# DLRM interaction tower on one core: the gathers of each feature group wait for a step of TensorE

## The chip, the core and the metric

The kernel runs on one core of a Trainium2 chip. The metric is the device time of one execution in microseconds (us), lower is better; the median of three runs is given. Engines: TensorE (PE) multiplies matrices, with its weight loads shown apart (PEld); VectorE (DVE), ScalarE (ACT) and GpSimd (POOL) work elementwise; SyncE (SP) and ScalarE also issue plain DMAs, and GpSimd issues the indirect ones, the gathers.

## The reference

For each of 2048 samples, 27 embedding rows of 128 floats are looked up, all pairs of them multiplied, and the result goes through a small MLP:

```python
e = jnp.stack([tbl_0[ids[:, 0]], ..., tbl_26[ids[:, 26]]], axis=1)   # (2048, 27, 128)
inter = einsum('bfd,bgd->bfg', e, e)                                  # 27 x 27 per sample
x = inter[:, lower triangle]                                          # 351 pairs
h = concatenate([bottom, x, bottom], axis=1)                          # (2048, 607)
h = maximum(h @ W_top1 + b_top1, 0)                                   # 512
h = maximum(h @ W_top2 + b_top2, 0)                                   # 256
y = h @ W_top3                                                        # (2048, 1)
```

The tables have 1000 to 125000 rows. Everything is float32.

## The kernel before

The 2048 samples are 16 tiles of 128, and two tiles make a half (256 samples, `h` from 0 to 7; the name is the kernel's). Tile `t` of half `h` is `2h` (even) or `2h + 1` (odd).

The ten smallest tables (1000 or 1250 rows) lie in SBUF, split in a rounded part `tab_hi` and a rest `tab_lo`. Their rows are not gathered but selected: VectorE builds a one-hot matrix from the indices (`one_hot`, line 536), TensorE multiplies the table's chunk with it (`select`, line 389). A **step** is one chunk of one set of tables, that is one one-hot and its 4 or 8 matmuls, and TensorE counts it in the semaphore `onehot_used`. Half 0 has 50 steps (sets of two tables or one), each later half 26 (two sets of four tables with 8 chunks, 8 matmuls a step; one set of two tables with 10 chunks, 4 matmuls a step), 168 selection matmuls in all. `OH_AT[h]` is the count of steps ahead of half `h`. Five one-hots can be ahead of TensorE.

The other 17 tables are gathered from HBM by GpSimd, one indirect DMA per tile and feature (128 rows of 512 bytes), 272 in all (line 359). The 17 features are in five groups of 3, 3, 4, 3, 4 (`GROUPS`), with first features 0, 3, 6, 10, 13. The buffer `emb` has two slots, so tile `t` goes where tile `t - 2` was, and group `g` of it waits until TensorE has transposed group `g` of tile `t - 2` (`is_filled(pool, "rows", t - TILE_SLOTS, g)`, line 357). Within GpSimd the gathers are issued strictly in order.

TensorE's program is an order written out by hand (from line 474). For a half from 2 on: the first two sets of `select` (128 matmuls); the transposes of the even tile, groups 0 to 3 (`rows`, line 401); the third set (40 matmuls); group 4; the transposes of the bottom input (line 425); layer 2 of the MLP for half `h - 2` (lines 459 to 461); the Gram products of the even tile (`products`, line 416, four steps of 32 matmuls, each counted in `grammed`); layer 3 for half `h - 2` (line 470); the transposes of the odd tile, groups 0 to 4; layer 1 for half `h - 1` (lines 442 to 444, 48 matmuls); the Gram products of the odd tile. The semaphore `filled` counts in this same order each bank of PSUM that TensorE has filled. Half 7 has no layer 1 in its place; the last layers follow the end of its Gram products.

ScalarE copies the selected and transposed rows to `embT` (lines 506 and 675) and the Gram products to `inter` (line 683); SyncE stores them to HBM and loads them back packed by pairs (lines 319 and 280). In half 0 the tables and weights are loaded and split, which ScalarE (642, 647) and VectorE (521, and 542 to 562 for the weights) do between the steps.

Of the kernel before, what the change touches and what calls it, by code (L numbers as in the profile page):

```python
# [34 lines left out]
def dlrm_tower(nc, bottom, ids, sel_ids, gather_tables, select_tables, w_top1, b_top1, w_top2, b_top2, w_top3, out):  # L35
# [20 lines left out]
    for f in range(1, NF):  # L56
        k, g = f * (f - 1) // 2, 0
        while g < f:
            n = min(f - g, P - k % P)
            PACKS.append((f, g, n, k // P, k % P))  # L60
            k, g = k + n, g + n
# [14 lines left out]
    for rows in shapes:  # L76
        of_shape = [i for i in range(NSEL) if select_tables[i].shape[0] == rows]
        FOURS += [(of_shape[a:a + 4],) + table_chunks(rows) for a in range(0, len(of_shape), 4)]
    K = FOURS[0][1]
    assert all(k == K for _, k, _ in FOURS) and all(four[-1] - four[0] == len(four) - 1 for four, _, _ in FOURS)  # L80
    CHUNKS = [table_chunks(t.shape[0])[1] for t in select_tables]
    CHUNK_AT = [sum(CHUNKS[:i]) for i in range(NSEL)]

    TWOS = [(four[a:a + 2], k, chunks) for four, k, chunks in FOURS for a in range(0, len(four), 2)]
    TWOS = TWOS[:1] + TWOS[-1:] + TWOS[1:-2] + [([i], k, chunks) for four, k, chunks in TWOS[-2:-1] for i in four]
    TABLE_ORDER = [i for two, _, _ in TWOS for i in two]


    PIECE = BANK // D
    PIECES = [(TABLE_ORDER.index(i), a, min(PIECE, CHUNKS[i] - a)) for two, _, chunks in TWOS for a in range(0, chunks, PIECE) for i in two]  # L90
    SPLIT_BY = [max(p for p, (x, _, _) in enumerate(PIECES) if x == n) + 1 for n in range(NSEL)]
    PIECES_OF = [[p for p, (n, _, _) in enumerate(PIECES) if TABLE_ORDER[n] in two] for two, _, _ in TWOS]
# [3 lines left out]
    OH_AT = [sum(len(one) for one in ONEHOTS[:h]) for h in range(HALVES + 1)]  # L96
    ROW_IDS = sorted({c for _, _, c in FOURS})
    ROW_AT = {c: sum(x for x in ROW_IDS if x < c) for c in ROW_IDS}
    GRAMS = P // QUADS // SPAN
# [64 lines left out]
    with ExitStack() as ctx:  # L164
# [3 lines left out]
        def sem(name):  # L168
            return ctx.enter_context(nc.semaphore(name))
# [74 lines left out]
        onehot_used = sem("onehot_used")  # L244
        filled = sem("filled")
        freed = [sem(f"freed_{b}") for b in range(BANKS)]
        grammed = sem("grammed")
# [15 lines left out]
        def is_filled(eng, *key):  # L263
            eng.wait_ge(filled, fill[key])
# [11 lines left out]
        def load_packs(eng, h, packs, loaded):  # L276

            both = grams[2 * h:2 * h + 2].rearrange("t s f g n -> (t s) f g n")
            for f, g, n, c, k in packs:
                eng.dma_start(packed[k:k + n, c, :].rearrange("k (s n) -> k s n", s=2 * QUADS),  # L280
                              both[:, f, g:g + n, :].rearrange("s k n -> k s n")).then_inc(loaded[c], 16)
# [60 lines left out]
        @block.gpsimd  # L342
        def _(pool):
            for c in ROW_IDS:
                pool.iota(row_id[:, ROW_AT[c]:ROW_AT[c] + c], pattern=[[1, c]], base=0, channel_multiplier=c).then_inc(row_id_ready, 1)
            pool.wait_ge(ident_zeroed, 1)
            pool.affine_select(out=ident[:, :], in_=ident[:, :], compare_op=ALU.not_equal, fill=1.0,
                               base=0, pattern=[[-1, P]], channel_multiplier=1).then_inc(ident_ready, 1)
            pool.wait_ge(ids_loaded[0], 16)
            for t in range(TILES):  # L350
                if t == 2:
                    pool.wait_ge(ids_loaded[1], 16)
                if t == ID_SLOTS:
                    pool.wait_ge(ids_loaded[2], 16)
                for g, features in enumerate(GROUPS):
                    if t >= TILE_SLOTS:
                        is_filled(pool, "rows", t - TILE_SLOTS, g)
                    for f in features:
                        pool.indirect_dma_start(  # L359
                            out=emb[:, t % TILE_SLOTS, f, :], out_offset=None, in_=gather_tables[f],  # L360
                            in_offset=bass.IndirectOffsetOnAxis(ap=ids_all[:, t % ID_SLOTS, f:f + 1].bitcast(U32), axis=0),
                        ).then_inc(gathered[t % TILE_SLOTS][g], 16)
            pool.wait_ge(packed_split, CH * (HALVES - 1))
            pool.wait_ge(stored, 16 * QUADS * TILES)
            load_packs(pool, HALVES - 1, POOL_PACKS, packs_pool)
# [447 lines left out]
```

## Time and profile before

| | |
|---|---|
| median of 3 runs | 382.04 us (380.87 to 382.43) |
| span of the profiled execution | 633.3 us |
| TensorE busy, in the profile | 402.0 us (63%), 4321 matmuls |
| TensorE weight loads | 374.0 us (59%) |
| VectorE | 254.0 us (40%) |
| ScalarE | 144.4 us (23%) |
| GpSimd | 262.1 us (41%) |
| mean granted TensorE clock | 0.827 of full |
| DMA | 45.76 MB, mean 72 GB/s |

No time from outside the profiler is listed for the profiled execution itself; its own time is the span of 633.3 us, which is 251 us longer than the median of the timed runs. So no share of the span may be taken for a share of the 382 us. A row of the timeline gives start, duration, engine, line, operation, output and inputs, and in brackets how long the engine was idle before and what ended that. "issue" there means that the engine waited for nothing that the profile shows.

### The profile page before, as it was taken

The numbers are of one execution on the slowest core, as the hardware profiler recorded it, in microseconds if no ns is written. First come the engines' busy times: TensorE is split into PE (matmuls) and PEld (weight loads), VectorE is DVE, ScalarE is ACT, GpSimd is POOL, SyncE is SP. The second block draws the span as 40 slices with busy tenths as digits, with TensorE's granted clock in tenths as the row PEclk, the third lists the DMA queues.
The fourth block names the chain that finished last, engine by engine and source line by source line (L and its number), as shares of the span: only waits on it lengthen the run. The fifth ranks groups of instructions, "written<-read, shape, count | busy, mean of one in ns | idle before, by whom it ended". The sixth has DMA issues, their size and how long they took to land.

```text
span 633.3 us, 10256 instructions
## 1 busy us (share of the span) xinstructions
PE 402.0 (63%) x4321; PEld 374.0 (59%) x4321; DVE 254.0 (40%) x341; ACT 144.4 (23%) x268; POOL 262.1 (41%) x283
## 2 busy tenths in 40 slices
PE   2207655492738928298465956469392892839997
PEld 2206543492727918197464955469381992829986
DVE  3117955191315704074040921338040560407422
ACT  3204722020302213112311123012130221311521
POOL 6761447317370364505463073712646045550010
PEclk9999967597668969599595996769776896959999
DMA  8812652114221232114121241211321132211021
GB/s 200 174 50 77 175 167 77 52 28 135 55 55 40 64 104 65 41 40 128 35 75 28 45 134 47 61 39 36 127 64 53 36 81 84 64 40 39 9 61 9
DMA packets 44889, 45.76 MB, mean 72 GB/s; under 512 B 32720, under 2 KB 35558, under 8 KB 43948
## 3 DMA queue, kind: packets, MB, share of 16 engines
q1 hardware_dynamic: 33646, 26.52, 16.3%
q0 software_dynamic: 8896, 17.89, 10.9%
q10 hardware_dynamic: 2302, 0.70, 0.5%
q8 instruction: 34, 0.56, 0.4%
q14 instruction: 11, 0.09, 0.0%
HBM read 39.52 MB, written 5.55 MB: 71 GB/s over the span
## 4 chain that ended last, share of the span: by engine, by line
PE 50%; issue 20%; another core or an unknown queue 18%; ACT 5%; DVE 4%; DMA 2%; SPq 0%; ACTq 0%; DVEq 0%
PE work L389 21%; PE gram L416 16%; PE work L401 3%; PE work L442 2%; PE work L443 2%; PE work L444 2%; DVE onehot L536 2%; ACT embT L506 2%; ACT embT L675 2%; DMA inter<-in_tbl 1%; PE work L470 1%; DVE tab_lo L521 1%; DMA misc<-in_bottom 1%; PE work L459 1%
## 5 line engine op out<-in xcount | busy, mean ns | idle before, releaser
L359 POOL DMA_INDIRECT emb<-in_tbl,ids_all x272 | 258.2, 949 | 304.9 <-PE work L401 217.7
L536 DVE TENSOR_TENSOR onehot<-ids_bc,row_idf 125x1024 fp32r<-125x1024 int32 (+2 forms) x232 | 199.4, 921 | 94.0 <-PE work L389 60.9
L416 PE MATMUL gram<-embT 128*54 128x52 f32 x2048 | 110.3, 264 | 161.7 <-issue 134.6
L389 PE MATMUL work<-onehot,tab_hi 125*128 125x256 f32 x672 | 172.8, 296 | 51.2 <-DVE onehot L536 26.0
L416 PEld LDWEIGHTS gram<-embT 128*54 128x54 f32 x2048 | 93.9, 179 | 181.5 <-issue 164.2
L389 PE MATMUL work<-onehot,tab_lo 125*128 125x256 f32 x672 | 169.2, 291 | 0.0
L389 PEld LDWEIGHTS work<-onehot,tab_hi 125*128 125x128 f32 x672 | 133.8, 199 | 57.0 <-DVE onehot L536 32.4
L389 PEld LDWEIGHTS work<-onehot,tab_lo 125*128 125x128 f32 x672 | 134.3, 200 | 0.0
L675 ACT COPY embT<-work 128x512 f32<-128x512 f32 (+1 forms) x41 | 30.4, 795 | 163.5 <-PE work L389 98.9
L569 DVE SCALAR_TENSOR_TENSOR x_lo<-work,x_hi 128x512 fp32r<-128x512 f32 x16 | 11.0, 691 | 103.9 <-ACT x_hi L708 72.6
L683 ACT COPY inter<-gram 118x416 f32<-118x416 f32 x64 | 32.3, 506 | 66.5 <-remote 33.6
L506 ACT COPY embT<-work 128x512 f32<-128x512 f32 (+1 forms) x64 | 36.4, 623 | 25.8 <-remote 16.5
L708 ACT ACTIVATE x_hi<-work 128x512 fp32r<-128x512 f32 x14 | 8.4, 597 | 144.7 <-remote 129.9
L442 PE MATMUL work<-x_hi,w_hi 128*128 128x256 f32 (+1 forms) x128 | 36.9, 288 | 0.8 <-DVE x_lo L601 0.8
L606 DVE TENSOR_TENSOR x_lo<-work,x_hi 128x256 fp32r<-128x256 f32 x8 | 3.4, 424 | 84.6 <-ACT x_hi L702 72.8
L443 PE MATMUL work<-x_lo,w_hi 128*128 128x256 f32 (+1 forms) x128 | 36.2, 283 | 0.0
L444 PE MATMUL work<-x_hi,w_lo 128*128 128x256 f32 (+1 forms) x128 | 36.2, 283 | 0.0
L401 PE MATMUL work<-ident,emb 128*128 128x128 f32 x272 | 35.8, 278 | 0.0
L401 PEld LDWEIGHTS work<-ident,emb 128*128 128x128 f32 x272 | 31.1, 145 | 0.9
L506 DVE COPY embT<-work 128x384 f32<-128x384 f32 x16 | 8.9, 559 | 46.1 <-PE work L401 45.0
L442 PEld LDWEIGHTS work<-x_hi,w_hi 128*128 128x128 f32 (+1 forms) x128 | 24.5, 191 | 1.1 <-DVE x_lo L601 1.0
L443 PEld LDWEIGHTS work<-x_lo,w_hi 128*128 128x128 f32 (+1 forms) x128 | 24.5, 192 | 0.0
(56 smaller groups left out, 220.9 us busy)
## 6 DMA issues: line engine op xcount, KB each, us to landing
ids_bc<-in_sel_ids SPq DMA_DIRECT2D x7, 1280.0 KB
grams<-inter SPq DMA_DIRECT2D x64, 84.5 KB
emb<-in_tbl,ids_all POOLq DMA_INDIRECT x272
misc<-in_tbl SPq DMA_DIRECT2D x3, 448.0 KB
inter<-in_tbl SPq DMA_DIRECT2D x3, 448.0 KB
ids_bc<-in_sel_ids SPq DMA_DIRECT2D x4, 256.0 KB, 5.2
misc<-in_bottom SPq DMA_DIRECT2D x8, 128.0 KB
raw_hi<-in_tbl SPq DMA_DIRECT2D x1, 560.0 KB
```

The costliest lines, as they stand in the source:

```text
L359: pool.indirect_dma_start(out=emb[:, t % TILE_SLOTS, f, :], out_offset=None, in_=gather_tables[f], in_offset=bass.IndirectOffsetOnAxis(ap= ...
L389: mm = nc.tensor.matmul(out, part[0:k, CHUNK_AT[f] + c, :], onehot[0:k, at % RING, i * HALF:(i + 1) * HALF], start=(c == 0 and i % 2 == 0 ...
L401: last = nc.tensor.transpose(out[:, j * P:(j + 1) * P], emb[:, t % TILE_SLOTS, f, :], ident[:, :])
L416: last = nc.tensor.matmul(gram[side * SIDE:side * SIDE + TWO * NF, n % 2, q, 0:COLS], two.rearrange("d s f -> d (s f)"), two[:, :, 0:NG], ...
L442: nc.tensor.matmul(out, w1_hi[0:k, c, cols], x_hi[0:k, at, :], start=(n == 0 and m % 2 == 0), stop=False, skip_group_check=True)
L443: nc.tensor.matmul(out, w1_hi[0:k, c, cols], x_lo[0:k, at, :], start=False, stop=False, skip_group_check=True)
L444: last = nc.tensor.matmul(out, w1_lo[0:k, c, cols], x_hi[0:k, at, :], start=False, stop=(n == CH), skip_group_check=True)
L506: copy(embT[:, t % 2, :, f:f + k], bank("rows", t, g)[:, 0:k * P].rearrange("d (f n) -> d n f", n=P)).then_inc(freeing("rows", t, g), 1)
L536: nc.vector.tensor_tensor(onehot[0:k, at % RING, 0:width], ids_bc[0:k, four[0]:four[-1] + 1, :].rearrange("p i n -> p (i n)"), row_idf[0:k ...
L569: nc.vector.scalar_tensor_tensor(out=x_lo[:, at:at + 2, :].rearrange("p m n -> p (m n)"), in0=bank("mlp1", h, b), scalar=0.0, in1=x_hi[:, ...
L675: nc.scalar.copy(embT[:, :, :, f:f + n], bank("select", h, j, b)[:, 0:n * HALF].rearrange("d (f i p) -> d i p f", f=n, p=P)).then_inc(free ...
L683: nc.scalar.copy(inter[0:ROWS, :, u * SPAN:(u + 1) * SPAN], gram[0:ROWS, n % 2, :, 0:COLS].rearrange("f q g -> f g q")).then_inc(extracted, 1)
```

## The change

Only GpSimd's program is edited. Ahead of the first gather of a group (the others of the group follow at once) stands a wait for a count that TensorE reaches in its own order:

- tile 0: none. Tile 1, in half 0: groups 0 to 4 wait for steps 8, 14, 20, 28 and 34 of half 0's 50.
- even tiles from 2 on, `2h + 2`, which are gathered from the middle of half `h`: group 0 nothing new; group 1 the 18th of the 26 steps of half `h` (from half 1 on); group 2 the bottom transposes of half `h`; group 3 the first Gram step of tile `2h`; group 4 the transposes of group 1 of tile `2h + 1`.
- odd tiles from 3 on, `2h + 3`: group 0 nothing new; group 1 the first Gram step of tile `2h + 1`; groups 2, 3 and 4 the steps 2, 7 and 11 of half `h + 1`.

The old waits for the buffers stay.

```diff
--- before.py
+++ after.py
@@ -346,6 +346,25 @@
             pool.wait_ge(ident_zeroed, 1)
             pool.affine_select(out=ident[:, :], in_=ident[:, :], compare_op=ALU.not_equal, fill=1.0,
                                base=0, pattern=[[-1, P]], channel_multiplier=1).then_inc(ident_ready, 1)
+
+            def behind_even(h, g):
+
+                if g == 1 and h:
+                    pool.wait_ge(onehot_used, OH_AT[h + 1] - 8)
+                elif g == 2:
+                    is_filled(pool, "bottom", h)
+                elif g == 3:
+                    pool.wait_ge(grammed, 2 * h * GRAMS + 1)
+                elif g == 4:
+                    is_filled(pool, "rows", 2 * h + 1, 1)
+
+            def behind_odd(h, g):
+
+                if g == 1:
+                    pool.wait_ge(grammed, (2 * h + 1) * GRAMS + 1)
+                elif g > 1:
+                    pool.wait_ge(onehot_used, OH_AT[h + 1] + (2, 7, 11)[g - 2])
+
             pool.wait_ge(ids_loaded[0], 16)
             for t in range(TILES):
                 if t == 2:
@@ -356,6 +375,10 @@
                     if t >= TILE_SLOTS:
                         is_filled(pool, "rows", t - TILE_SLOTS, g)
                     for f in features:
+                        if f == features[0] and t == 1:
+                            pool.wait_ge(onehot_used, 8 + 2 * f)
+                        elif f == features[0] and t > 1:
+                            (behind_odd if t % 2 else behind_even)(t // 2 - 1, g)
                         pool.indirect_dma_start(
                             out=emb[:, t % TILE_SLOTS, f, :], out_offset=None, in_=gather_tables[f],
                             in_offset=bass.IndirectOffsetOnAxis(ap=ids_all[:, t % ID_SLOTS, f:f + 1].bitcast(U32), axis=0),
```

On the other engines the instructions are the same. GpSimd's row before, tile 1 from its first gather (the first half; `in_tbl_N` is the table that is gathered from):

```order
L359 DMA emb<-in_tbl_2,ids_all 128x128
L359 DMA emb<-in_tbl_3,ids_all 128x128
L359 DMA emb<-in_tbl_5,ids_all 128x128
L359 DMA emb<-in_tbl_6,ids_all 128x128
L359 DMA emb<-in_tbl_8,ids_all 128x128
```

And with the change, the same gathers of tile 1 and the two after them:

```order
L382 DMA emb<-in_tbl_2,ids_all 128x128 [waits onehot_used]
L382 DMA emb<-in_tbl_3,ids_all 128x128
L382 DMA emb<-in_tbl_5,ids_all 128x128
L382 DMA emb<-in_tbl_6,ids_all 128x128 [waits onehot_used]
L382 DMA emb<-in_tbl_8,ids_all 128x128
L382 DMA emb<-in_tbl_10,ids_all 128x128
L382 DMA emb<-in_tbl_13,ids_all 128x128 [waits onehot_used]
```

Tiles 0 and 1 were issued as one row of 34 without a wait; now each group of tile 1 begins with one. GpSimd's row before at tile 5, an odd one, from its first gather (`filled`: the transposes that free the buffer):

```order
L359 DMA emb<-in_tbl_2,ids_all 128x128 [waits filled]
L359 DMA emb<-in_tbl_3,ids_all 128x128
L359 DMA emb<-in_tbl_5,ids_all 128x128
L359 DMA emb<-in_tbl_6,ids_all 128x128 [waits filled]
L359 DMA emb<-in_tbl_8,ids_all 128x128
L359 DMA emb<-in_tbl_10,ids_all 128x128
L359 DMA emb<-in_tbl_13,ids_all 128x128 [waits filled]
```

With the change, from the same gather of tile 5 on:

```order
L382 DMA emb<-in_tbl_2,ids_all 128x128 [waits filled]
L382 DMA emb<-in_tbl_3,ids_all 128x128
L382 DMA emb<-in_tbl_5,ids_all 128x128
L382 DMA emb<-in_tbl_6,ids_all 128x128 [waits grammed,filled]
L382 DMA emb<-in_tbl_8,ids_all 128x128
L382 DMA emb<-in_tbl_10,ids_all 128x128
L382 DMA emb<-in_tbl_13,ids_all 128x128 [waits onehot_used,filled]
```

The gathers keep their order; groups 1 and 2 of the tile now also wait for a Gram step and for a selection step of the next half. Where the added wait is one for `filled` (groups 2 and 4 of even tiles), it takes the place of the old one in the list, with a higher count.

## Rows read from the trace of the kernel before

**Rows 1.** The page's head.
```profile
span 633.3 us, 10256 instructions
```
**Rows 2.** Waits: engine, line, what was waited for, us in total, times, longest.
```profile
POOL emb L359 <- PE work L401: 217.7, 17, 24.5
PE gram L416 <- issue: 134.6, 121, 12.9
```
**Rows 3.** Instructions of line 359: count, duration in ns as min/median/max.
```profile
L359 POOL DMA_INDIRECT emb<-in_tbl,ids_all x272: 941/947/1585, 2.9 to 563.6; - x136
```
**Rows 4.** Timeline of GpSimd: start us, us, instruction, idle before it and its releaser.
```profile
2.89 1.18 POOL L359 DMA_INDIRECT emb<-in_tbl,ids_all  x1 [1.43 <-DMA ids_all<-in_ids]
...
44.43 0.95 POOL L359 DMA_INDIRECT emb<-in_tbl,ids_all  x1 [0.31 <-issue]
...
367.39 0.95 POOL L359 DMA_INDIRECT emb<-in_tbl,ids_all  x1 [0.30 <-issue]
```
**Rows 5.** Windows: PE, PEld, DVE, ACT, POOL busy (count), PEclk, DMA, GB/s.
```profile
272.34:346.98 74.64, 49.82 (x542) 46.79 (x541) 28.37 (x34) 15.36 (x30) 32.16 (x34) 0.79 0.24 64
...
401.00:417.90 16.90, 3.38 (x26) 2.44 (x23) 0.69 (x1) 0.60 (x1) 10.47 (x12) 0.60 0.18 47
```
**Rows 6.** Chain that ended last, in order of time: start us, us, what.
```profile
123.19 16.19 PE work L389 x128
...
572.31 15.56 PE work L389 x128
...
597.97 3.35 PE gram L416 x128
...
602.30 1.93 PE work L401 x17
```
**Rows 7.** Timeline of TensorE, half 7: its second Gram stage.
```profile
605.36 3.41 PE L416 MATMUL gram<-embT 128*54 128x52 f32 x128 [1.14 <-ACT embT L506]
```
**Rows 8.** Timeline of TensorE, first and last of 48 matmuls of layer 1.
```profile
319.19 0.36 PE L442 MATMUL work<-x_hi,w_hi 128*128 128x256 f32 x1
...
324.90 0.28 PE L444 MATMUL work<-x_hi,w_lo 128*128 128x256 f32 x1
```
**Rows 9.** Timeline of TensorE in half 0, around the two long stops.
```profile
20.57 0.41 PE L389 MATMUL work<-onehot,tab_lo 125*128 125x256 f32 x1
46.62 0.55 PE L389 MATMUL work<-onehot,tab_hi 125*128 125x256 f32 x1 [25.63 <-DVE onehot L536]
...
98.42 1.43 PE L416 MATMUL gram<-embT 128*54 128x52 f32 x44 [0.80 <-DVE embT L506]
```
**Rows 10.** TensorE in half 0: steps 13, 19, 27, 31, then the stages behind.
```profile
54.04 0.55 PE L389 MATMUL work<-onehot,tab_hi 125*128 125x256 f32 x1 [3.50 <-DVE tab_lo L521]
...
60.22 0.35 PE L389 MATMUL work<-onehot,tab_hi 125*128 125x256 f32 x1 [0.18 <-DVE tab_lo L521]
...
67.64 0.36 PE L389 MATMUL work<-onehot,tab_hi 125*128 125x256 f32 x1 [0.91 <-DVE tab_lo L521]
...
71.37 0.36 PE L389 MATMUL work<-onehot,tab_hi 125*128 125x256 f32 x1 [1.23 <-DVE tab_lo L521]
...
86.64 0.69 PE L425 MATMUL work<-ident,misc 128*128 128x128 f32 x2 [1.47 <-DMA misc<-in_bottom]
90.82 4.79 PE L416 MATMUL gram<-embT 128*54 128x52 f32 x128 [3.50 <-issue]
95.55 2.08 PE L401 MATMUL work<-ident,emb 128*128 128x128 f32 x17
```
**Rows 11.** DMA issues: count, KB each, us from issue to landing.
```profile
raw_lo<-in_W_top SPq DMA_DIRECT2D x2, 256.0 KB, 2.7
```
**Rows 12.** Timelines of GpSimd and VectorE: the longest gather and what ran beside.
```profile
98.87 1.58 POOL L359 DMA_INDIRECT emb<-in_tbl,ids_all  x1 [0.30 <-issue]
...
98.42 1.23 DVE L562 TENSOR_TENSOR w_lo<-raw_hi,w_hi 128x1024 fp32r<-128x1024 f32 x1
```

## Prediction

> **What bounds the kernel now.** I read the head of the page first, then the times. The profiled execution spans 633.3 us [rows 1]; the median of the timed runs is 382.04 us. The 251 us between them decide what a saving seen in the profile is worth, so they come first.
>
> The list of waits names them. GpSimd waits 217.7 us for TensorE's transposes, and TensorE loses 134.6 us in front of the Gram matmuls to "issue", that is to nothing that the profile shows [rows 2]. GpSimd's own instruction is steady: 272 gathers, median 947 ns [rows 3], and 0.30 us between them [rows 4], so 1.25 us from one to the next, 21.3 us for a tile's 17 and 42.5 us for a half's 34. The windows show where TensorE loses its time: from 401.0 to 417.9 GpSimd gathers and TensorE does 26 matmuls at a granted clock of 0.60 [rows 5]. The same 128 Gram matmuls take 3.35 us at 597.97, with no gather in flight [rows 6]. I call such a stretch a freeze: while gathers follow each other without a gap, the other engines stand nearly still.
>
> Is the freeze in the timed runs? I take it out and sum.
> - A half without it: the last one, from 572.31 [rows 6] to the end of its second Gram stage at 605.36 + 3.41 = 608.77 [rows 7], 36.46 us. It lacks the mlp1 stage, 319.19 to 325.18, 5.99 us, less its shadow over the 1.14 us that TensorE waits for ScalarE there [rows 7, 8]. Sum 41.3 us; a half under the profiler took 74.64 [rows 5].
> - The start, up to half 1 at 123.19 [rows 6]. TensorE stands for 25.63 us before 46.62, of which I leave 1; the second Gram stage runs from 98.42 to 123.19 where 4.1 would do (3.4 at the full clock, some more at its start) [rows 9]. So 123.2 - 24.6 - 20.7 = 77.9.
> - The end: 633.3 - 572.3 = 61.0.
> - 77.9 + 6 x 41.3 + 61.0 = 386.7 us, against 633.3 measured with the freeze and a median of 382.04 without the profiler. The sum without any freeze is already 4.7 us too long. So the timed runs hold next to none of it, and TensorE, in its written order, sets their time.
>
> The Trainium skill speaks to this ("NOTIFIC — the notification-queue block", 7.1 Overflow): the block that writes trace records holds its producers back internally instead of losing a record. By that rule the freeze is made by the tracing and pacing gathers cures only profiles. The difference of 251 us between the profile and the median agrees; no row names the cause.
>
> **The change.** No instruction is added on TensorE, VectorE, ScalarE or SyncE, and the 272 gathers stay in order. What is new is 60 waits on GpSimd: 5 for tile 1, 3 for tile 2, 4 for each of tiles 3 to 15 (that is 24 and 28). A met wait costs nothing visible: gathers that carry one in a running burst show the same 0.30 us [rows 4], so 60 x 0 to 60 x 0.01 us, on an engine that doesn't set the end. Behind a waiting gather stand only later gathers; for those wait TensorE's transposes. So the change costs what it makes the transposes late, and brings what gathers now disturb.
>
> How late the gathers get, in the freeze-free time of above (profile times of the first half less 24.6).
> Before. GpSimd issues tiles 0 and 1 from 2.89 without a gap [rows 4] until 45.7. Tile 2 ends at 67. Tile 3 needs the transposes of tile 1, 95.55 - 24.6 = 71.0 [rows 10], and ends at 92.5. Tile 4 needs the first group of tile 2's transposes, 15.8 us into half 1, 93.7; from there twelve tiles at 21.3 run on end to end, since 42.5 us of gathers meet a half of 41.3. The last gather is issued at 93.7 + 255 = 349.
> After. Tile 1's groups wait for steps 8, 14, 20, 28, 34. From the starts of steps 13, 19, 27 and 31 (54.04, 60.22, 67.64, 71.37 [rows 10]) these end at about 21, 31, 37, 44 and 49. The last group is out at 49.1 + 5.0 = 54.1, not 45.7. Tile 2's third group waits for the bottom transposes (86.64 + 0.69 - 24.6 = 62.7), the fourth for the first Gram step (92.0 - 24.6 = 67.4, met), the fifth for a transpose of tile 1 (71.7) [rows 10]; it ends at 76.7. Tile 3 follows at once: the Gram step of 75, and steps 2, 7, 11 of half 1 (79.8, 84.7, 88.6, at 15.6/16 us a step) are past when GpSimd gets there (80.5, 84.3, 89.3, 93.0), but for 0.4 us at step 7. It ends at 98.0. From there GpSimd again has more to do than a half is long, and the waits are met when it comes to them. The last gather is issued at 98.0 + 255 = 353.
> Needed. Half 7 starts at 77.9 + 6 x 41.3 = 325.7; the last group of tile 15 is transposed 30.0 us in (602.30 - 572.31 [rows 6]) plus 1.5, at 357.2. Slack at issue 8.2 us before, 4.2 after. A gather's landing isn't in the rows; the nearest row is that of two 256 KB loads of weights, which land 2.7 us after issue [rows 11]. 1.5 us are left: TensorE doesn't wait, and the term is 0. All earlier tiles have more.
>
> Freed on the other side: in the first 50 us tile 1's gathers no longer run in one piece beside the loads of the tables. In the profile TensorE waits there for VectorE's tab_lo between pieces, 1.2 us at a time [rows 10], and that is paced by VectorE, not by a load. Between 0 and the 1.2 us of one such wait, I take 0.
>
> One rule speaks against the change. One gather took 1585 ns [rows 3]: it starts at 98.87, beside VectorE's subtraction of two SBUF inputs from 98.42, 1.23 us long [rows 12]. The gathers beside one-hots, one SBUF input and one in PSUM, stay at 947. The Trainium skill ("SBUF — State Buffer", Who interferes with whom) says the same: VectorE with two SBUF inputs contends with a GpSimd instruction that reads SBUF, and the later one blocks; the trace agrees in this one place. The change moves tile 2's last seven gathers onto VectorE's splitting of the weights, at 0.64 us for each that meets one: at most 4.5 us of GpSimd's time, by the rule the slack is gone; with two or three met, it isn't.
>
> Sum: 0 on TensorE's path in the freeze-free time, and 382.0 us.
>
> **Rivals.**
> A. *GpSimd becomes late.* My sum is 4.7 us above the median. If that error lies in the six halves, not in the start, half 7 comes 4.7 us earlier, the slack of 1.5 turns to -3.2, and every microsecond goes to the end: 385.2 us, with two blocked gathers 386.5. For it: 42.5 against 41.3 us a half. Against: it needs gathers without the profiler as slow as with it; 1% off the cadence over the last 204 gathers returns 2.6 us. It decides from 1.5 us of further lateness, at the transposes of tile 15, line 401.
> B. *Part of the freeze is real.* Then spreading the gathers gives back time that my sum doesn't see. A freeze is 74.6 - 41.3 = 33.3 us a half; 3% of that, 1 us, over seven halves is 7 us: 375 us. For it: the granted clock falls to 0.60 in the freeze [rows 5], which is a real thing in that execution. Against: the sum leaves it no room.
> C. *The change does nothing in timed runs*, because GpSimd lags behind each step anyway. That is most of my forecast, with the same number.
>
> **Numbers.** Forecast (C in it) 0.55, A 0.23, B 0.22. The likeliest alone: 380.5 to 383.7, which is the runs shown (380.87 to 382.43) and the 1.2 us. About 0.5% (1.9 us) is what a measurement of this kernel tells from no change. With A to 386.5 and half of B, the range is 376.5 to 386.5. Faster by over 0.5%: B less what of it is small, and a little of the forecast's edge, 0.22. Slower: A, 0.24. Same: 0.54.
>
> **What would show it.** Right: in the new profile no group of tile 15 is waited for by line 401, and outside the freezes the stages keep their lengths (15.6 us for 128 selection matmuls, 3.4 for a Gram stage). The profile's span may fall far, towards 450 to 600 us, since GpSimd now stops while TensorE stands, and so hands it time back; that would be a gain under the profiler alone. Wrong: a time below 380, and then the freeze was in the timed runs; or above 384, with line 401 waiting for GpSimd's queue.

## The result

The change makes the kernel slower by a little. Over 11 runs each on one chip: 383.91 us (382.75 to 386.19) against 382.43 us (380.87 to 383.41); the ratio is 1.0062, 95% interval 1.0039 to 1.0086. Two later comparisons of the same two kernels (`e9_after_again`, `e15_after_third`) gave 1.0067 (1.0041 to 1.0093) and 1.0077 (1.0048 to 1.0105). Where a run took over 1.5% more than the fastest of its kernel (one of the six of `e7_waits_tiles1_2`), the ratios leave it out.

That is the answer for one kind of chip only. The chips on which the experiments ran fall in two kinds: in four comparisons (the first one among them) the kernel before took 382 us, in two 634 to 639 us, run after run. By its length, the profile that stands before the prediction (633.3 us) is from a chip of the second kind, while the times beside it (382 us) are from one of the first. On the second kind the change is a large gain, 0.8264 (0.8151 to 0.8377). Below, "382-chip" and "634-chip" are the two kinds. The five comparisons after the first ran on five different chips, each once; so it is not shown that a chip stays of its kind at another time.

**The profile after, on a 382-chip.** Its head, and rows of parts 1 and 2 (tenths busy in 40 slices):

```profile
span 384.3 us, 10311 instructions
...
PE 345.5 (90%) x4321; PEld 333.0 (87%) x4321; DVE 252.7 (66%) x341; ACT 142.9 (37%) x268; POOL 263.1 (68%) x283
...
PE   0668666999899999999999999999999999997996
...
POOL 6776476777777777777777777777777777773030
PEclk9979966999999999999999999999999999999898
```

From the eighth slice on TensorE is busy at 0.9 or more and at the full clock, but for single slices and the last few: no trace of the freeze. GpSimd's row of sevens is 0.95 us of every 1.25 us: it gathers without a pause. The list of waits, the rows that answer to [rows 2]:

```profile
POOL emb L382 <- issue: 69.2, 227, 0.3
...
POOL emb L382 <- PE work L412: 11.4, 20, 2.7
...
PE gram L439 <- issue: 3.7, 1, 3.7
...
PE work L424 <- DMA emb<-in_tbl,ids_all: 2.3, 2, 1.4
```

The last row is the new one: twice TensorE waits for a gather to land. (The lines are those of the changed file: 382 is the gather, 424 the transposes, 439 the Gram products, 412 the selection.) The chain that ended last shows both places, and the halves between them:

```profile
72.98 17.02 PE work L412 x128
...
113.37 15.55 PE work L412 x128
...
154.37 15.55 PE work L412 x128
...
277.78 15.55 PE work L412 x128
...
307.39 2.96 DMA emb<-in_tbl,ids_all
...
320.15 15.55 PE work L412 x128
...
349.90 3.06 DMA emb<-in_tbl,ids_all
```

Half 1 starts at 73.0, half 7 at 320.2. A half takes 41.0 us (154.37 - 113.37), and 42.4 where tile 13's last group is awaited (320.15 - 277.78). The last gather of tile 15 starts at 349.90 and has landed 3.06 us later. TensorE there:

```profile
350.00 1.62 PE L424 MATMUL work<-ident,emb 128*128 128x128 f32 x13
353.00 0.66 PE L424 MATMUL work<-ident,emb 128*128 128x128 f32 x4 [1.38 <-DMA emb<-in_tbl,ids_all]
354.71 4.99 PE L439 MATMUL gram<-embT 128*54 128x52 f32 x128 [1.05 <-ACT embT L529]
```

Groups 0 to 3 of tile 15 are transposed in one piece, then TensorE waits 1.38 us for group 4. The kernel before, profiled again on a 382-chip (run `e13_before_third` below), is the one to compare with, not [rows 2] to [rows 10]. Its timelines of GpSimd (first gathers of tiles 3 and 4, last of tile 15) and of TensorE:

```profile
68.51 0.94 POOL L359 DMA_INDIRECT emb<-in_tbl,ids_all  x1 [1.68 <-PE work L401]
91.75 0.95 POOL L359 DMA_INDIRECT emb<-in_tbl,ids_all  x1 [1.63 <-PE work L401]
...
346.19 0.95 POOL L359 DMA_INDIRECT emb<-in_tbl,ids_all  x1 [0.30 <-issue]
```
```profile
350.25 2.05 PE L401 MATMUL work<-ident,emb 128*128 128x128 f32 x17
353.35 3.41 PE L416 MATMUL gram<-embT 128*54 128x52 f32 x128 [1.05 <-ACT embT L506]
```

Before, GpSimd waits for a buffer at tile 3 and at tile 4, so it is up to date there, starts tile 4 at 91.8 and issues its last gather at 346.2, and the 17 transposes of tile 15 run in one piece. With the change tile 4 starts at 95.5 (in the other profiles of the same kernel at 95.6 and 97.1), and the last gather at 349.9: 3.7 us later at both ends, with 254 us of gathers between them that have no gap. Against TensorE it is later by more. By its first matmul, half 1 starts at 74.0 in this profile of before and at 72.9 in that of the change; the other two profiles of the changed kernel have it at 73.1 and 74.6, so that is scatter and not the change. Measured from the first transpose of tile 2, which frees the buffer, tile 4's first gather is 0.8 us late before and 5.7 us with the change: 4.9 us more.

### The profile page after: what moved, and what is told of

The parts are those of the page before. It is cut to its first block, busy times and chain, and to the rows that moved or that the text cites. A ratio compares the mean times of both kernels' runs of the same rounds, so it can differ in the third digit from the quotient of the medians.

```text
span 384.3 us, 10311 instructions
## 1 busy us (share of the span) xinstructions
PE 345.5 (90%) x4321; PEld 333.0 (87%) x4321; DVE 252.7 (66%) x341; ACT 142.9 (37%) x268; POOL 263.1 (68%) x283
## 4 chain that ended last, share of the span: by engine, by line
PE 80%; DVE 6%; DMA 5%; issue 3%; POOL 3%; ACT 2%; SPq 1%
PE work L412 40%; PE gram L439 14%; PE work L424 7%; PE work L465 4%; PE work L466 4%; PE work L467 4%; DVE onehot L559 4%; POOL emb L382 3%; DVE tab_lo L544 2%; DMA inter<-in_tbl 2%; PE work L482 2%; PE work L484 2%; PE work L483 2%; DMA emb<-in_tbl,ids_all 2%; PE work L493 1%
## 5 line engine op out<-in xcount | busy, mean ns | idle before, releaser
L382 POOL DMA_INDIRECT emb<-in_tbl,ids_all x272 | 259.2, 953 | 90.1 <-issue 69.2
L412 PEld LDWEIGHTS work<-onehot,tab_hi 125*128 125x128 f32 x672 | 132.1, 197 | 30.7 <-issue 18.2
L412 PEld LDWEIGHTS work<-onehot,tab_lo 125*128 125x128 f32 x672 | 132.6, 197 | 0.0
L439 PEld LDWEIGHTS gram<-embT 128*54 128x54 f32 x2048 | 56.1, 136 | 10.0 <-issue 7.4
L439 PE MATMUL gram<-embT 128*54 128x52 f32 x2048 | 58.1, 219 | 7.3 <-issue 3.7
L467 PEld LDWEIGHTS work<-x_hi,w_lo 128*128 128x128 f32 (+1 forms) x128 | 24.5, 191 | 0.0
L482 PE MATMUL work<-x_hi,w_hi 128*128 128x256 f32 x64 | 18.7, 293 | 0.0
```

Source lines behind the costliest of these rows:

```text
L382: pool.indirect_dma_start(out=emb[:, t % TILE_SLOTS, f, :], out_offset=None, in_=gather_tables[f], in_offset=bass.IndirectOffsetOnAxis(ap= ...
L412: mm = nc.tensor.matmul(out, part[0:k, CHUNK_AT[f] + c, :], onehot[0:k, at % RING, i * HALF:(i + 1) * HALF], start=(c == 0 and i % 2 == 0 ...
L439: last = nc.tensor.matmul(gram[side * SIDE:side * SIDE + TWO * NF, n % 2, q, 0:COLS], two.rearrange("d s f -> d (s f)"), two[:, :, 0:NG], ...
L467: last = nc.tensor.matmul(out, w1_lo[0:k, c, cols], x_hi[0:k, at, :], start=False, stop=(n == CH), skip_group_check=True)
L482: nc.tensor.matmul(out, w2_hi[:, c, cols], x_hi[:, at, :], start=(c == 0), stop=False)
```

## The experiments

Theory L: waits make GpSimd start tile 4's gathers late; since from there it has more work a half than a half is long, it never catches up, and the last transposes wait. Rival W: the waits cost by themselves, or by where they put the gathers. Rival S: gathers fall on the loads of the tables. For each kernel the first gather of tile 4 (`tile 4 at`) is read from GpSimd's timeline, in us from the start of the span. The diffs are cut to the lines that change; line numbers shift from kernel to kernel.

**Is it GpSimd's lateness?** Four gathers (5.0 us of GpSimd's work) are left out of the kernel before and of the changed one, in the middle of the run.

```diff
+LEFT_OUT = [(8, 2)]
...
-                    for f in features:
+                    for f in features if (t, g) not in LEFT_OUT else []:
```

The pair is tile 8, group 2. The wait of the transposes is lowered to match (that line is not shown); they transpose the rows of tile 6 again for this group. Before:

> The kernel before, leaving out the four gathers of group 2 of tile 8 (TensorE transposes the rows of tile 6 again there). This takes 5.0 us of work off GpSimd and nothing off TensorE. Theory L: before, GpSimd ends some 5 us earlier than after and no transposes wait, so the time stays at 382.4 within 0.6. If GpSimd binds already before, it falls by 1 us or more.

Measured: 382.73 us, ratio 1.0015 (0.9995 to 1.0035): nothing. With the change:

> The changed kernel, leaving out the same four gathers of group 2 of tile 8. All 60 waits stay. Theory L: GpSimd is 5.0 us earlier from tile 9 on as far as the waits allow (they bind at about 1 to 3 us), tiles 13 and 15 are waited for no longer: 380 to 382. Rival W (the waits cost by themselves, or by where they put the gathers): 383.9 as the change.

Measured: 381.80 us, ratio to before 1.0008 (0.9988 to 1.0028). All 60 waits are still there, tile 4 is still 5.7 us late, no transposes wait at the end, and the loss is gone. So GpSimd's work limits the changed kernel and not the one before, as theory L has it. Rival W's 383.9 is not seen.

**Which waits make GpSimd late?** First without the five of tile 1:

```diff
-                        if f == features[0] and t == 1:
-                            pool.wait_ge(onehot_used, 8 + 2 * f)
-                        elif f == features[0] and t > 1:
+                        if f == features[0] and t > 1:
```

> The changed kernel without the five waits of tile 1; those of tiles 2 to 15 stay. Theory L (GpSimd is late: its gathers run without a gap from tile 2 to the end, and the last groups of tiles 13 and 15 land after TensorE wants them): tile 2 still waits for the bottom transposes and the first Gram step of half 0, so its end stays near 74 us of the profile and nothing is won: 383.5 to 384. Rival S (the waits of tile 1 shift gathers onto the loads of the tables): 382.4, as before. If the 633 us span of the profile before comes from the one piece of 34 gathers at the start alone, the span here is long again.

Measured: 384.54 us, 1.0076 (1.0046 to 1.0106), tile 4 at 95.3. The whole loss is still there, which also rules out rival S. GpSimd's timeline says why; tile 2's third group:

```profile
58.06 0.94 POOL L380 DMA_INDIRECT emb<-in_tbl,ids_all  x1 [5.23 <-PE work L446]
```

The 5.2 us that tile 1 no longer loses, tile 2 waits for the bottom transposes. Then only the waits of tile 1:

```diff
-                        elif f == features[0] and t > 1:
-                            (behind_odd if t % 2 else behind_even)(t // 2 - 1, g)
```

> The kernel before with only the five waits of tile 1. Theory L: tile 2 ends at about 72 instead of 67, tile 3 at 93 instead of 88.5; tile 4 can start at 90.4 at the earliest, so GpSimd is 2.8 us later than before from there on; the slack of before is some 1.5 us, so 382.8 to 384. Rival S: the whole +1.5 us, 383.9. If only the first piece of 34 gathers makes the profile long, its span is near 384 here.

Measured: 382.59 us, 1.0024 (1.0007 to 1.0041), tile 4 at 93.2. A third of the loss.

These two expectations also asked whether the piece of 34 gathers makes the profile long. Both spans were short (382.2 and 380.3 us), and so was that of `e3_before_less_4_gathers`, which has the 34 gathers in one piece. So that piece alone isn't the cause. The kernel before once more:

> The kernel before once more, nothing changed: the time must be that of before within 0.3%. The question is its profile. If the span of 633 us was a matter of that one execution, it is near 380 us here, TensorE stands nowhere for longer than some 13 us at the start, GpSimd issues tile 4 from about 91 us, ends tile 15 at about 346, and no transposes of tiles 13 or 15 wait for a gather. If the freeze belongs to the kernel before under the profiler, it is near 630 again.

Measured, on another chip: 633.82 us against 634.93 for the same kernel, 0.9994 (0.9975 to 1.0013). The profiled execution took 633.55 us, no more than the others. The three kernels that follow ran on this chip too, and then again on a 382-chip. Without the eight waits of tiles 1 and 2:

```diff
-                        if f == features[0] and t == 1:
-                            pool.wait_ge(onehot_used, 8 + 2 * f)
-                        elif f == features[0] and t > 1:
+                        if f == features[0] and t > 2:
```

> The change without the eight waits of tiles 1 and 2: the 52 waits of tiles 3 to 15 stay. Theory L (only the late start of tile 4's gathers counts, and that comes from half 0): tile 3 begins near 68, tile 4 near 91, all as before, so the time is that of before within 0.6 us. Rival W (each wait costs, or spreading costs): most of the +2 us stays.

On the 634-chip: 530.93 us, 0.8365 (0.8335 to 0.8395). Again:

> The change without the eight waits of tiles 1 and 2. On a chip where before takes 382: theory L expects the time of before within 0.6 us, since tile 4 begins at 91 us as before; rival W expects +2. On a chip where before takes 634: 531 again.

On a 382-chip: 382.17 us, 0.9996 (0.9975 to 1.0017), tile 4 at 90.1. So 52 of the 60 waits cost nothing that is seen. The other eight alone:

```diff
-                        elif f == features[0] and t > 1:
-                            (behind_odd if t % 2 else behind_even)(t // 2 - 1, g)
+                        elif f == features[0] and t == 2:
+                            behind_even(0, g)
```

> Only the eight waits of tiles 1 and 2, the 52 others gone. Theory L: tile 2 ends at 74, tile 4 begins at 95.5, as in the change, and the last gathers of tile 15 are awaited for 1 to 1.5 us: +1.5 to +2.8 us, as the change. Rival W: as before.

On the 634-chip: 622.36 us, 0.9791 (0.9763 to 0.9819).

> Only the eight waits of tiles 1 and 2. On a chip where before takes 382: theory L expects the whole loss of the change, +1.5 to +2.8, with tile 15 awaited; rival W as before. On a chip where before takes 634: 622 again.

On a 382-chip: 384.51 us, 1.0068 (1.0046 to 1.0091), tile 4 at 96.3: the whole loss of the change. And with the waits of tile 1 but not the three of tile 2 (the change with `t > 2` for `t > 1` in the second condition):

> The change without the three waits of tile 2 (57 stay). On a chip where before takes 382: theory L expects tile 4 at about 93, as with the waits of tile 1 alone, so +0.3 to +1.5 us, clearly less than the change. On the other kind: between 450 and 531 us, since tile 1's one piece of 17 gathers is broken up too.

On a 382-chip: 383.66 us, 1.0032 (1.0010 to 1.0054), tile 4 at 93.9; between.

**Does lateness alone do it?** The kernel before, with one wait and nothing else:

```diff
+                    if (t, g) == (4, 0):
+                        pool.wait_ge(onehot_used, OH_AT[2])
                     for f in features:
```

> The kernel before with one wait: the first gather of tile 4 waits for the last step of half 1, so it begins at about 97 instead of 91. Theory L: all later gathers are 6 us later, 1 us of that is slack, so +4 to +5 us. Rival W or no bound by GpSimd: the time of before, since tile 4 itself is needed only at 129.

On the 634-chip: 637.78 us, 1.0037 (1.0020 to 1.0054).

> The kernel before with the first gather of tile 4 held until the last step of half 1. On a chip where before takes 382: theory L expects tile 4 at 97 instead of 91, all later gathers 6 us later, +4 to +5 us; rival: no loss. On a chip where before takes 634: 638 again.

On a 382-chip: 386.81 us, 1.0118 (1.0090 to 1.0145), +4.8 us. Its waits:

```profile
PEld work L403 <- DMA emb<-in_tbl,ids_all: 4.4, 3, 1.9
PE work L403 <- DMA emb<-in_tbl,ids_all: 3.7, 3, 1.6
```

The tile that was held is wanted only at 127.8 us and comes in time; the transposes that wait are the last groups of tiles 11, 13 and 15, some 170 us later and more. Tile 4 starts at 96.4 here, earlier than in one profile of the change (97.1), and the loss is still the largest. What orders the kernels is how late GpSimd is against TensorE. The table has, for the profiles on 382-chips, tile 4's first gather behind the first transpose of tile 2, and the time from the start of half 1 to the end of the span, which leaves out the scatter of the start:

| kernel | tile 4 late by, us | half 1 to the end, us | ratio to before |
|---|---|---|---|
| before (e13) | 0.8 | 307.3 | 0.9993 |
| before less 4 gathers (e3) | 0.8 | 306.9 | 1.0015 |
| waits from tile 3 on (e10) | 0.8 | 306.7 | 0.9996 |
| waits of tile 1 alone (e2) | 4.4 | 308.3 | 1.0024 |
| change without tile 2's waits (e14) | 4.4 | 308.5 | 1.0032 |
| change without tile 1's waits (e1) | 5.6 | 309.1 | 1.0076 |
| waits of tiles 1 and 2 (e11) | 5.6 | 309.6 | 1.0068 |
| the change (e9, e15) | 5.6, 5.7 | 309.5, 309.6 | 1.0067, 1.0077 |
| the change, first profile | 5.7 | 311.4 | 1.0062 |
| before, tile 4 held (e12) | 7.5 | 311.8 | 1.0118 |
| change less 4 gathers (e4) | 5.7 | 306.9 | 1.0008 |

The later tile 4 is, the longer the rest takes, and without the four gathers it isn't longer though tile 4 is as late. The first profile of the change is longer than its two others by a slow Gram stage (last section).

**The two kernels again, and the floor.**

> The changed kernel itself, beside before on the same chip. Chips differ: on one the kernel before takes 382 us, on another 634, and the profile before (633.3) belongs to the second kind. On a chip of the first kind: +2 us, 384. On one of the second kind theory B (the freeze is real there, and groups of gathers with gaps end it in part) expects 440 to 530 us, below the 531 of the kernel with the waits of tiles 3 to 15 alone; theory P (the change only matters under special conditions of the profile) expects 634.

On a 382-chip: 384.72 us, 1.0067, tile 4 at 95.6.

> The kernel before, unchanged, for its profile. On a chip where it takes 382 us, theory L expects: tile 4's gathers from 90 to 91 us, tile 15's last one issued by 346 to 347, and landed (3 us) just ahead of the transposes, so no row of line 401 waiting for a gather for more than 0.5 us. On the other kind of chip 634 us.

On a 382-chip: 381.72 us, 0.9993 (0.9969 to 1.0017); its rows are shown above. No transposes wait.

> The changed kernel. On a chip where before takes 382: +2 to +2.8 us again. On the other kind: theory B expects 440 to 531 us, a gain of 16 to 30%; if tile 2's waits hurt there as well, 520 to 540.

On a 382-chip: 385.45 us, 1.0077, tile 4 at 97.1, the last group of tile 15 awaited for 1.24 us. For the floor, the kernel before without the gathers of tiles 2 to 15 (the wait of the transposes is lowered to match, and they transpose the rows of tiles 0 and 1 again):

```diff
-                    for f in features:
+                    for f in features if t < TILE_SLOTS else []:
```

> The kernel before, leaving out all gathers of tiles 2 to 15 (TensorE transposes the rows of tiles 0 and 1 again). Theory G (gathers hold the other engines on some chips, and nothing else does): 378 to 382 on a chip of the first kind, since TensorE's own order sets the time there; some 400 on one of the second kind, where only the 24 us stop at the start is left. If something else than the gathers holds the engines there, it stays above 550.

On a 382-chip: 381.54 us, 0.9980 (0.9958 to 1.0002). With 238 of 272 gathers gone the kernel gains 0 to 0.4%: on such a chip TensorE's own order sets the time of before, and no order of those gathers could have gained more than that.

**On a 634-chip.** The changed kernel:

> The changed kernel. On a chip where before takes 382: 384 to 385.5. On one where it takes 634: 440 to 540 by theory B.

Measured: 528.28 us (2 runs) against 639.07 (3 runs), 0.8264 (0.8151 to 0.8377). And the kernel before without the gathers of tiles 2 to 15:

> The kernel before, leaving out all gathers of tiles 2 to 15. On a chip where before takes 382: 381.5. On one where it takes 634: some 405 if gathers alone hold the other engines, above 550 if something else does.

Measured: 409.45 us (2 runs), 0.6405 (0.6372 to 0.6438). Its chain shows halves of 41.0 us, as on the other chips:

```profile
141.26 15.55 PE work L389 x128
...
182.26 15.55 PE work L389 x128
...
305.64 15.55 PE work L389 x128
...
346.64 15.55 PE work L389 x128
```

So on that chip the gathers of tiles 2 to 15 cost 639.07 - 409.45 = 230 us, on a 382-chip at most 1.6 (e16). Of what remains above 381.5, 28 us, all lies in the first half, where the 34 gathers of tiles 0 and 1 still run: half 1 starts at 100.9 instead of 72.2. TensorE has one long stop there:

```profile
50.29 0.55 PE L389 MATMUL work<-onehot,tab_hi 125*128 125x256 f32 x1 [29.56 <-DVE tab_lo L521]
```

That these 34 gathers make this stop is likely, and was not tested by leaving them out. With the change on that chip, the windows of a stretch of about one half (391.0 to 450.6) and of a part of it:

```profile
391.00:450.60 59.60, 49.84 (x534) 46.97 (x529) 29.08 (x34) 14.38 (x30) 32.15 (x34) 0.89 0.31 81
405.00:417.00 12.00, 10.29 (x82) 9.53 (x81) 8.14 (x8) 1.47 (x2) 6.91 (x8) 1.00 0.28 64
```

Against [rows 5]: about a half in 59.6 us instead of 74.6, TensorE busy for 10.3 of the 12 us in which GpSimd issues 8 gathers, instead of 3.4 of the 16.9 in which it issues 12. GpSimd's waits there are real pauses, for example 2.24 us:

```profile
414.59 0.95 POOL L382 DMA_INDIRECT emb<-in_tbl,ids_all  x1 [0.31 <-issue]
417.78 0.95 POOL L382 DMA_INDIRECT emb<-in_tbl,ids_all  x1 [2.24 <-PE work L424]
```

## Why the prediction was wrong

It said no change, 382.0 us, in a range of 376.5 to 386.5 that held the time; the change is slower beyond its interval. The mechanism was named, as rival A, with a chance of 0.23 and the price 385.2 us; measured were 383.9 to 385.5. So the term for what GpSimd's lateness costs TensorE was put at 0 and is some 2.5 us, and one inference beside it was false.

**The step that failed: the slack of tile 15, "1.5 us are left: TensorE doesn't wait, and the term is 0".** It is the difference of two times, each from a long sum:
- Needed: I put half 7 at 325.7 and the last group at 357.2. Measured, 320.2 and 351.6 (350.00 + 1.62). The halves were nearly right (41.0 against 41.3, and one of 42.4 with the wait of tile 13 in it); the start was not, 73.0 instead of 77.9. Taking the two long stops out of a start that holds gathers as well did not give the start of a 382-chip.
- Arrived: I put tile 4's first gather at 98.0 and the last one's issue end at 353. Measured 95.5 and 350.8. The cadence (21.3 us a tile, 255 for twelve) was right.
- The landing: I added 2.7 us to the end of the issue; measured 2.1 (349.90 + 3.06 - 350.84).

The need is 5.6 us earlier, the arrival 2.2 us, the landing 0.6 us: 1.5 - 5.6 + 2.2 + 0.6 = -1.3, and the wait is 1.38 us. "All earlier tiles have more" failed too: tile 13 is awaited for 0.9 us. The delays are somewhat longer than the waits: half 6, with tile 13 in it, takes 42.4 us instead of 41.0, and from the start of half 7 to its last Gram stage 34.6 us pass instead of 33.0 (e13): 1.4 and 1.6 us. In e9 they are 1.1 and 1.3, in e15 1.7 and 1.5. That is the loss, 0.62 to 0.77% of 382 us or 2.4 to 2.9 us, as near as single profiles can tell.

Set against before, both terms behind the slack were off: before, the last gather lands 2.6 us ahead of its use (346.19 + 3.06 against 350.25 + 1.62), not 5.5 (8.2 less the 2.7 of the landing), and the change makes the gathers 4.9 us later against TensorE, not 4.0. I had seen that the sum stood 4.7 us above the median and that an error in the halves would turn the slack. I took the start for the safer place of the error. It is not safe there either: GpSimd's chain hangs only in part on the start, the need wholly. When the margin (1.5 us) is smaller than the known error of the sum (4.7 us), the rival that lives in this margin deserves at least the forecast's chance.

**The cost outside tile 15.** "A met wait costs nothing visible": right, 52 waits together give 0.9996. The path that I wrote down for half 0 (tile 1 to 54.1, tile 2 to 76.7, tile 4 at 98) has the right shape: 50.6, 74.0, 95.5 were measured. The removal experiments put the loss where that path has it, in the eight waits of tiles 1 and 2, and show what the prediction did not see: they don't add up. Without tile 1's waits the whole loss stays (e1), since tile 2 then waits the longer for the bottom transposes; without tile 2's waits a third to a half of it stays (e2, e14).

**VectorE's weight splitting.** I allowed up to seven gathers at 0.64 us each and wrote that two or three leave some slack. For three that was wrong by its own numbers: 1.92 us is more than 1.5. In the profile after, three there were longer:

```profile
64.29 1.20 POOL L382 DMA_INDIRECT emb<-in_tbl,ids_all  x1 [0.74 <-PE gram L439]
...
68.30 1.20 POOL L382 DMA_INDIRECT emb<-in_tbl,ids_all  x1 [0.30 <-PE work L424]
69.80 1.66 POOL L382 DMA_INDIRECT emb<-in_tbl,ids_all  x1 [0.30 <-issue]
```

Together 0.25 + 0.25 + 0.71 = 1.2 us over a normal gather, nearly as much as the 1.38 us that tile 15 lacks. What the Trainium skill says ("SBUF — State Buffer", Who interferes with whom) was worth a term of its own here. That VectorE causes these three was not tested; each runs beside a subtraction of the weights' splitting, at 64.70 and 69.41. The kernel before has such gathers as well, one of 1.59 us at 71.01 in e13, but there tile 4 has to wait 1.63 us for its buffer anyhow. With the change GpSimd no longer waits for a buffer there, so nothing takes up what they cost.

**The freeze.** Rightly used: the timed runs hold none of it, and the sum without it came within 1.2%. Wrongly explained: I put it down to the tracing. The same profiler shows spans of 379 to 384 us on the 382-chips, so tracing alone doesn't make it, and on a 634-chip the profiled execution takes what the other runs take. With that the guess on the new profile ("450 to 600 us, a gain under the profiler alone") failed: the new profile has 384.3 us because it is from a 382-chip, and on a 634-chip, where the span with the change is 523.6 us, the runs that were timed gain as well. What the Trainium skill says of the block that writes the records ("NOTIFIC — the notification-queue block", 7.1 Overflow) does not explain the difference; no run here shows that block holding an engine. The list of runs has a granted clock for each of them, so none is known to have run without records, and a part of the tracing on 634-chips alone is not ruled out.

Rival B had the right effect for the other kind of chip. On the 634-chips spreading the gathers gives back 111 us; on the one that was timed there was nothing to give back, as e16 shows.

**A version for both kinds** is the change without the waits of tiles 1 and 2 (e6, e10): 0.9996 of before on a 382-chip, where the change has 1.0067 on the same chip, and 0.8365 on a 634-chip, where the change has 0.8264 on another one; those two intervals overlap.

**Left open.** Why the chips differ, or whether it is the chip at all and not something else that differed between the comparisons, and by what a run of gathers holds the other engines on some of them. Gathers of another size, or the same gathers from another queue, were not tried there.

## What to carry to other kernels

A wait that costs nothing where it stands can cost at the far end: once an in-order engine has more work per period (42.5 us) than the period is long (41.0), a microsecond lost early is still missing at the last tile, less the slack there (2.6 us here), and the place to look is where its last product is needed. When span and timed median differ by more than a few per cent, profile the unchanged kernel beside timed runs on the same chip, before any argument rests on either. And a margin is worth only as much as the error of the two sums that it is the difference of.

## What the runs showed of the hardware

- Trainium2 chips ran this program in 382 us or in 634 to 639 us, each steadily while it was used (22 to 29 runs of before in each of four comparisons, within 1.1%). Most of the difference needs the gathers: 409.45 us without those of tiles 2 to 15, where a 382-chip takes 381.54.
- GpSimd itself isn't slowed there: 1.25 us from gather to gather on both kinds.
- The granted clock fell once behind a stop of 1.38 us, 0.66 us of transposes and a second stop of 1.05 us. In the profile of the change the 128 Gram matmuls after that take 4.99 us instead of 3.41; the windows of that stretch and of the same stretch in `e15_after_third`, whose first stop was 1.24 us:

```profile
354.70:361.20 6.50, 6.49 (x141) 6.44 (x142) 0.00 (x0) 2.03 (x4) 0.00 (x0) 0.74 0.03 7
```
```profile
356.20:360.00 3.80, 3.76 (x131) 3.74 (x132) 0.00 (x0) 1.82 (x4) 0.00 (x0) 1.00 0.02 4
```

  In the first the granted clock falls from 2.4 to 1.2 GHz for a part (mean 0.74), in the second it stays. In eight profiles on 382-chips the last group of tile 15 is awaited, for 1.08 to 1.64 us; the clock fell in this one alone, and not behind the longest stop (`e1_no_tile1_waits`):

```profile
352.54 0.66 PE L422 MATMUL work<-ident,emb 128*128 128x128 f32 x4 [1.64 <-DMA emb<-in_tbl,ids_all]
354.25 3.41 PE L437 MATMUL gram<-embT 128*54 128x52 f32 x128 [1.05 <-ACT embT L527]
```

  So the length of the stop alone doesn't decide it. The fall cost 1.6 us in the profile where it came; how often it comes in the other runs, and so its share of the median loss, is not shown. A run's mean clock doesn't tell: on one chip two runs of before with 0.965 and 0.987 took 382.24 and 382.19 us.
- Gathers are longer beside VectorE instructions that add or subtract two SBUF tiles. In the twelve profiles on 382-chips with all or nearly all gathers, every gather of over 1.0 us but the very first overlaps one, in the weights' splitting or in that of the MLP's input (`x_lo`); 5 to 9 of the 14 to 19 that overlap one are that long, the longest 1.83 us. No run took the VectorE instructions away.
